# A transformer block on one core: token tiles combined in pairs, and the last sequence's weighted sums moved to TensorE

## The reference, cut to what matters

```
h = layernorm(x) * (1 + cb) + sb
top_logits, top_idx = top_k(h @ gate_w, 2)          # two experts per token
top_w = softmax(top_logits)
y_e   = silu(h @ w1[e]) @ w2[e]                     # for the two experts of a token
x = x + gb * (top_w[0] * y_first + top_w[1] * y_second)
```

## Time and profile before

| what | value |
|---|---|
| median of three executions | 990.87 us (990.5 to 992.32) |
| span of the profiled execution, first to last instruction | 985.5 us |
| mean granted TensorE clock | 0.975 |
| TensorE busy | 890.2 us (90%) |
| VectorE busy | 712.9 us (72%) |
| ScalarE busy | 580.1 us (59%) |
| GpSimd busy | 350.7 us (36%) |
| DMA, mean over the span | 112 GB/s |

### The profile page before, as it was taken

The page is one execution under the profiler, slowest core; times in us unless marked ns, Lnnn a source line. Parts: engine busy times, 40 slices in busy tenths (PEclk is TensorE's granted clock), DMA queues, the critical chain, the costliest instruction groups (busy, mean ns, idle before and its releaser), DMA issues.

```text
span 985.5 us, 19308 instructions
## 1 busy us (share of the span) xinstructions
PE 890.2 (90%) x6090; PEld 529.1 (54%) x6164; DVE 712.9 (72%) x2285; ACT 580.1 (59%) x1268; POOL 350.7 (36%) x311
## 2 busy tenths in 40 slices
PE   7899899998899999989999987888899999999990
PEld 4443335433535434544443453432798899999880
DVE  7898776879566889657689668899547575444588
ACT  3335676766676777586676757757535433333563
POOL 4200030530430324323023444024585465565530
PEclk8998999999999999999999999999999999999996
DMA  6484535525506336253464565105332323222699
GB/s 204 122 176 108 79 110 111 91 72 98 79 1 144 68 79 144 76 70 95 73 123 105 127 114 180 36 26 177 110 97 76 96 73 105 73 81 75 194 313 306
DMA packets 83235, 110.61 MB, mean 112 GB/s; under 512 B 15930, under 2 KB 56434, under 8 KB 83138
## 3 DMA queue, kind: packets, MB, share of 16 engines
q1 hardware_dynamic: 75234, 88.40, 38.2%
q0 software_dynamic: 6816, 18.62, 6.0%
q10 hardware_dynamic: 1088, 2.36, 0.6%
HBM read 69.42 MB, written 35.41 MB: 106 GB/s over the span
## 4 chain that ended last, share of the span: by engine, by line
PE 64%; DVE 17%; ACT 9%; issue 6%; POOL 3%; DMA 1%; another core or an unknown queue 1%; SPq 0%; ACTq 0%; DVEq 0%; POOLq 0%
PE PY L1608 10%; PE PO L1741 9%; PE PH L1608 9%; PE PM L1698 9%; PE PS L1721 8%; ACT PR L1073 3%; PE PHT L1826 3%; DVE MXF L1410 3%; DVE JK L1407 3%; PE PX L1753 2%; PE PX L1662 2%; PE PS L1725 2%; PE PX L1673 1%; PE PX L1770 1%; POOL SF L912 1%
## 5 line engine op out<-in xcount | busy, mean ns | idle before, releaser
L1073 ACT ACTIVATE PR<-PS 128x512 f32<-128x512 f32 (+3 forms) x768 | 335.3, 499 | 125.6 <-PE PS L1725 85.6
L1407 DVE CUSTOM_DVE_ANT_0 JK<-PM,MK 128x128 bf16<-128x128 f32 (+3 forms) x512 | 239.5, 485 | 54.9 <-PE PM L1698 52.5
L1698 PE MATMUL PM<-QK 128*128 128x512 bf16 (+3 forms) x725 | 234.3, 332 | 22.9 <-DVE MXF L1410 11.6
L1721 PE MATMUL PS<-QK 128*128 128x512 bf16 (+3 forms) x737 | 235.0, 330 | 11.7 <-ACT PR L1073 9.2
L1410 DVE TENSOR_REDUCE MXF<-PM 128x1 f32<-128x512 f32 x256 | 175.2, 684 | 76.8 <-PE PM L1698 61.0
L1721 PEld LDWEIGHTS PS<-QK 128*128 128x128 bf16 x768 | 75.5, 99 | 167.2 <-ACT PR L1073 105.3
L1741 PE MATMUL PO<-PR,V 128*17 128x512 f32 (+3 forms) x1536 | 162.3, 495 | 0.2 <-DVE MXA L1407 0.2
L1698 PEld LDWEIGHTS PM<-QK 128*128 128x128 bf16 x768 | 75.5, 98 | 94.7 <-DVE MXF L1410 33.6
L1608 PE MATMUL PY<-W2S,HT 128*128 x852 | 119.4, 289 | 2.6 <-issue 1.8
L1725 PE MATMUL PS<-MT,identb 128*128 128x128 bf16 x512 | 111.4, 220 | 1.6 <-issue 0.8
L1608 PE MATMUL PH<-W1S,XT 128*128 x426 | 111.7, 397 | 0.6 <-DVE W2S L1562 0.6
(11 more groups left out here) (282 smaller groups left out, 1159.2 us busy)
## 6 DMA issues: line engine op xcount, KB each, us to landing
QK<-SD SPq DMA_DIRECT2D x180, 128.0 KB
SD<-SP SPq DMA_DIRECT2D x42, 256.0 KB, 2.9
OP<-OS SPq DMA_DIRECT2D x64, 64.0 KB
LP<-LR SPq DMA_DIRECT2D x64, 64.0 KB
W1S<-in_w SPq DMA_DIRECT2D x8, 512.0 KB, 6.6
X<-XA SPq DMA_DIRECT2D x3, 1024.0 KB, 8.4
H2D<-XA SPq DMA_DIRECT2D x3, 1024.0 KB, 4.8
YG<-YT SPq DMA_DIRECT2D x12, 256.0 KB
```

The costliest lines, as they stand in the source:

```text
L1073: eng.activation(PR[:, slot, i, c0:512], PS[m % 3][:, c0:512], ACT.Exp, scale=0.25).then_inc(S["exp"].sem, 1)
L1407: eng.tensor_tensor_reduce(JK[:, jk % 2, 0:w], PM[m % 3][:, 0:w], MK[:, 512 - w:512], 1.0, -3.0e38, ALU.add, ALU.max, MXA[:, mb, h, qt:qt ...
L1698: eng.matmul(PM[m % 3][:, 0:128 * (k1 - k0)], QK[:, r, h, 0, qt * 128:(qt + 1) * 128], QK[:, r, h, 1, k0 * 128:k1 * 128], start=True, stop ...
L1721: last = eng.matmul(PS[m % 3][:, c0:512], QK[:, r, h, 1, j * 128:(j + 1) * 128], QK[:, r, h, 0, 512 * f + c0:512 * f + 512], start=True, s ...
```

## The change

Token tiles are taken in pairs for the combine: n now counts pairs, 0 to 11 for sequences 0 to 2 (`LAST` = 12) and 12 to 15 for the last one. One transfer reads the residual rows of both tiles (256 KB), one the four expert rows (512 KB), one writes both (256 KB). ScalarE and VectorE's weighted steps stay one instruction for each tile, the gate product and the residual sum cover both tiles at once (128x512). The ring has 5 buffers for pairs. The keys are new: `gat(n)` 58.5 + n, `comb(n)` 60 + n, `out_st(n)` 60.5 + n.

For the last sequence all residual rows come in one transfer (`xrl`, 1 MB, key 71), ScalarE builds 16 diagonal matrices with the weights (`diag`, key 73), and TensorE forms the weighted sums with them, four fp32 matmuls of 256 columns for each pair, into PSUM banks that the expert part has left; VectorE then does only the gate product and the residual sum. The four gathers of expert rows have key 74.

```diff
-    for n in range(3 * NT):
-        place(NL + 2.5 + 0.6 * n, one("gat", n))
-        place(NL + 4.5 + 0.6 * n, combine(n))
-    for n in range(3 * NT, B * NT):
-        place(NF + 2, one("gat", n))
-        place(NF + 8 + n - 3 * NT, combine(n))
+    for n in range(LAST):
+        place(NL + 2.5 + n, one("gat", n))
+        place(NL + 4 + n, combine(n))
+    place(NF, one("xrl"))
+    place(NF + 2, one("diag"))
+    for n in range(LAST, LAST + PAIR_N):
+        place(NF + 3, one("gat", n))
+        place(NF + 8 + n - LAST, combine(n))
...
-RING = 10
+RING = 5
+PAIR_N = NT // 2
+LAST = (B - 1) * PAIR_N
...
 SyncE, gat(n):
-                    sp.wait_ge(S[f"x2{b}"], 16)
-                    if RING <= n < 3 * NT:
+                    if RING <= n < LAST:
                         sp.wait_ge(*after(f"o{r}", "out_st", n - RING))
-                    if n == 3 * NT:
-                        sp.wait_ge(*after("fh", "up", NF - 1))
-                    eng.dma_start(XR[r][:, :], X2[b, 128 * (n % NT):128 * (n % NT) + 128, :]).then_inc(S[f"yg{r}"].sem, 16)
-                    store_wait(sp, NL if n < 3 * NT else NF)
-                    eng.dma_start(YG[r][:, :, :], YT[EMPTY + 256 * n:EMPTY + 256 + 256 * n, :].rearrange("(k p) d -> p k d", p=128)
+                    if n < LAST:
+                        sp.wait_ge(S[f"x2{b}"], 16)
+                        eng.dma_start(XR[r], pair_rows(X2, n)).then_inc(S[f"yg{r}"].sem, 16)
+                    store_wait(sp, NL if n < LAST else NF)
+                    eng.dma_start(YG[r], YT[EMPTY + 512 * n:EMPTY + 512 + 512 * n, :].rearrange("(k p) d -> p k d", p=128)
                                   ).then_inc(S[f"yg{r}"].sem, 16)
+                elif kind == "xrl":
+                    sp.wait_ge(S[f"x2{B - 1}"], 16)
+                    sp.wait_ge(*after("fh", "up", NF - 1))
+                    eng.dma_start(XRL[:, :, :], x2_tiles(B - 1)).then_inc(S["xrl"].sem, 16)
...
 ScalarE:
+                    for t in range(2):
+                        eng.activation(YG[r][:, 2 * t, :], YG[r][:, 2 * t, :], ACT.Copy,
+                                       scale=TW[:, 0, 2 * n + t:2 * n + t + 1]).then_inc(S["cmb_a"].sem, 1)
+                elif kind == "diag":
+                    ac.wait_ge(*after("wt", "weights", 1))
+                    ac.wait_ge(*after("fh", "up", NF - 1))
+                    for n in range(NT):
+                        for k in range(2):
+                            eng.activation(DG[:, n, k, :], ident[:, :], ACT.Copy,
+                                           scale=TW[:, k, 2 * LAST + n:2 * LAST + n + 1]).then_inc(S["dg"].sem, 1)
...
 VectorE, comb(n):
+                    if some:
+                        dv.wait_ge(*after("cmb_a", "comb", n))
+                        for t in range(2):
+                            eng.scalar_tensor_tensor(out=YG[r][:, 2 * t, :], in0=YG[r][:, 2 * t + 1, :], ...)
+                        dv.wait_ge(S["comb"], c + 2)
+                    else:
+                        dv.wait_ge(*after("wsum", "comb", n))
+                        dv.wait_ge(S["xrl"], 16)
+                    eng.tensor_tensor(first, first if some else WS[n - LAST].rearrange("p (t d) -> p t d", t=2), gate,
+                                      ALU.mult).then_inc(sem, 1)
+                    dv.wait_ge(*after("comb", "comb", n))
+                    eng.tensor_tensor(XR[r], first, XR[r], ALU.add).then_inc(S["cmb_d"].sem, 1)
...
 TensorE:
+                elif kind == "comb" and a[0] >= LAST:
+                    pe.wait_ge(*after("dg", "diag"))
+                    pe.wait_ge(*after(f"yg{r}", "gat", n))
+                    for t in range(2):
+                        for k in range(2):
+                            last = eng.matmul(WS[i][:, 256 * t:256 * t + 256], DG[:, 2 * i + t, k, :], YG[r][:, 2 * t + k, :],
+                                              start=(k == 0), stop=(k == 1))
+                    last.then_inc(S["wsum"].sem, 1)
```

More of the change, by code:

```diff
@@ L393 @@
     "ystore": {f"ys{i}": (lambda t, i=i: 16 * (t % 4 == i)) for i in range(4)},
-    "gat": {f"yg{i}": (lambda n, i=i: 32 * (gat_ring(n) == i)) for i in range(RING + NT)},
-    "comb": {"cmb_a": 1, "comb": 2, "cmb_d": lambda n: int(n not in LATE), "cmb_p": lambda n: int(n in LATE)},
-    "out_st": {f"o{i}": (lambda n, i=i: 16 * (gat_ring(n) == i)) for i in range(RING + NT)},
+    "gat": {f"yg{i}": (lambda n, i=i: (32 if n < LAST else 16) * (gat_ring(n) == i)) for i in range(RING + PAIR_N)},
+    "xrl": {"xrl": 16},
+    "diag": {"dg": 2 * NT},
+    "comb": {"cmb_a": lambda n: 2 * (n < LAST), "wsum": lambda n: int(n >= LAST), "comb": lambda n: 3 if n < LAST else 1, "cmb_d": 1},
+    "out_st": {f"o{i}": (lambda n, i=i: 16 * (gat_ring(n) == i)) for i in range(RING + PAIR_N)},
 }
@@ L539, in adaln_block @@
         end = ExitStack()
-        YG = [sb(f"YG{i}", [128, 2, D], F32, end) for i in range(4)]
-        XR = [sb(f"XR{i}", [128, D], F32, end) for i in range(4)]
+        YG = [sb(f"YG{i}", [128, 4, D], F32, end)[:, :, :] for i in range(2)]
+        XR = [sb(f"XR{i}", [128, 2, D], F32, end)[:, :, :] for i in range(2)]
         G3R = G3[:, :, :, :].rearrange("p b t n -> p (b t) n")
-        YG += [XB[:, 3 * i:3 * i + 2, :] for i in range(2)] + [G3R[:, 3 * i:3 * i + 2, :] for i in range(4)]
-        XR += [XB[:, 3 * i + 2, :] for i in range(2)] + [G3R[:, 3 * i + 2, :] for i in range(4)]
+        YG += [XB[:, 0:4, :], G3R[:, 0:4, :], G3R[:, 6:10, :]]
+        XR += [XB[:, 4:6, :], G3R[:, 4:6, :], G3R[:, 10:12, :]]
         end.close()
@@ L552, in adaln_block @@
         last = ExitStack()
-        YG += [sb(f"YGL{i}", [128, 2, D], F32, last) for i in range(NT)]
-        XR += [sb(f"XRL{i}", [128, D], F32, last) for i in range(NT)]
+        YG += [sb(f"YGL{i}", [128, 4, D], F32, last)[:, :, :] for i in range(PAIR_N)]
+        XRL = sb("XRL", [128, NT, D], F32, last)
+        XR += [XRL[:, 2 * i:2 * i + 2, :] for i in range(PAIR_N)]
+        DG = sb("DG", [128, NT, 2, 128], F32, last)
         last.close()
@@ L569, in adaln_block, with results @@
         pff.close()
+        WS = [PX[:, :], PXT[:, :, :].rearrange("p a n -> p (a n)"), PH[0][:, :], PH[1][:, :]]
+        def results(r, k):
+            return YG[r].rearrange("p (t k) d -> p t k d", k=2)[:, :, k, :]
         CD = nc.dram_tensor("CD", [NG, 96, 128], BF16).ap()
@@ L864, in gpsimd_program @@
             const = S["const"].sem
-            done = {n: 0 for n in ("const", "sub_p", "neg_p", "gbo", "div_p", "om", "bias", "h2", "both", "cmb_p")}
+            done = {n: 0 for n in ("const", "sub_p", "neg_p", "gbo", "div_p", "om", "bias", "h2", "both")}
             newest = []
@@ L1149, in scalar_program @@
                     eng.activation(YO[:, t % 4, :], PY[t % 2][:, 0:256], ACT.Copy).then_inc(S["yo_a"].sem, 1)
-                elif kind == "comb":
+                elif kind == "comb" and a[0] < LAST:
                     n = a[0]
```

46 lines of the change are left out of this document (19 added, 27 removed).

## The result

The changed kernel took 1003.74 us (median of four, 1000.16 to 1005.87), the kernel before 990.68 us (median of four beside it). The ratio is 1.013, 95% interval 1.0107 to 1.0152: slower by 13 us. The forecast was slower by 6.0 us, 996.9 us, with a range that ended at 1002.0. Direction and mechanism were right, the size was under half of what was measured.

What follows compares the result with a forecast made beforehand. TensorE's expert tiles, then some 24 us of combine, were taken to set the end. Adding 10.5 us for late expert tiles and taking off 4.5 for a shorter tail gave +6.0 us, 996.9 us; range 986.4 to 1002.0.

Steps and rivals of the forecast that it cites:

- What the pairs save: Combine: VectorE needs 2.4 us for a pair instead of 2.6; counted at nothing while TensorE is the bound.
- What the new order costs: Combine loop: a round trip of 8.6 us against two beats, 6.96 us, makes a beat 4.3 us instead of 3.48.
- issue to landing: Combine loop: time from the issue of a pair's 512 KB gather until it lands, taken as 4.3 us.
- The signs that the prediction named: Changed timeline: `up(t)` every 4.2 to 4.4 us, ScalarE waiting for `YG<-YT`, TensorE idle some 8 us.
- the bound from above: Combine loop: upper estimate for a 512 KB gather's landing, from loaded 256 KB gathers, 5.3 to 6.2 us.
- The DMA rate as a reason of its own: Combine loop: a beat moves 1.05 + 0.26 MB, 3.8 us at 345 GB/s, already over 3.48.
- Where that puts the expert tiles: End of the expert tiles: last `down` ends at 971.8 us against 961.25 before, 10.5 us late.
- The tail: Behind the last `down`: scatter, gathers, TensorE's four pairs and store take 19.7 us instead of 24.2.
- From span to time: Whole run: 5.4 us added to the trace's end at 991.5 us gives a run's time, 996.9 us.
- number 4: Loop landings near the upper rows, 5.3 us, giving 1001.9 us, or tail clock staying low, 1001.4; chance 0.23 together.

Runs made afterwards that it cites:

- experiment 10: Changed kernel with a lead of four pairs and 34 dummy matmuls between the last `down` and the first diagonal matmul: 988.21 us, ratio 1.0005.
- experiment 7: Changed kernel with the twelve pairs' residual reads and result stores shrunk to 16 bytes a row, output of three sequences left out: 997.9 us, ratio 1.0089.
- experiment 11: experiment 10 with the last sequence's 1 MB of residual rows issued one place earlier in SyncE's list: 985.36 us, ratio 0.9975 to the kernel before.
- experiment 8: experiment 6 with 32 dummy matmuls between the last `down` and the first diagonal matmul: 993.37 us, ratio 1.0053 to the kernel before.
- experiment 6: Changed kernel with a pair combined every 1.2 beats and 3.6 beats of lead: 994.93 us, ratio 1.0061 to the kernel before.

## Why the prediction was right or wrong

**What the pairs save:** right in size. VectorE's group for a pair measures 0.88 us for the two weighted sums and 0.69 for each of the 128x512 instructions, 2.3 us with gaps. It brought nothing that shows: against 2.6 us for two single tiles it saves 0.3 us in a round trip of 10.

**What the new order costs:** the mechanism was right, and two experiments show it from both sides: one pair more of lead takes 8 us off the changed kernel, and a shorter lead alone puts 12 us on the old one. The step that failed is one term of the sum for the round trip, "issue to landing", put at 4.3 us. It measured 5.8 us in the mean. With it the round trip is 0.9 + 5.8 + 3.4 = 10.1 us, and the trace has it so: `comb(0)` ends at 925.57 and `comb(10)` at 976.40, five round trips of 10.2; `comb(1)` at 930.09 and `comb(11)` at 979.57, five of 9.9. Forecast were 926.3 and 969.3, 929.8 and 972.8. The starts were right within 0.8 us, and the 1.5 us of the term, five times over, are the 7 us at the end.

```profile
924.88 0.69 DVE L1623 TENSOR_TENSOR XR<-YG,XR 128x512 f32<-128x512 f32 x1
...
975.71 0.69 DVE L1623 TENSOR_TENSOR XR<-YG,XR 128x512 f32<-128x512 f32 x1
```

These are the last instructions of `comb(0)` and `comb(10)`. The signs that the prediction named came out accordingly: `up(t)` comes every 4.65 us in the mean from `up(60)` to `up(70)`, in steps of 3.2 to 8.7 us, instead of every 4.2 to 4.4; TensorE's waits for VectorE are 14.2 us instead of some 8; ScalarE does wait for DMA `YG<-YT`.

Why the term was short: I took the fixed part of a transfer, 1.4 us, from a 128 KB write into DRAM, and it does not hold for a gather from `YT`. In the tail the first 512 KB, with three more of its kind behind it, lands 987.76 - 983.74 = 4.0 us after its issue; if the bytes take 1.5 us, 2.5 are fixed, by this estimate. No run separates the two parts. The experiment without stores and residual rows has 4.5 in the loop. The row that I had put down as the bound from above (5.3 to 6.2 us, from the loaded gathers of the earlier trace rows) was the one that held. I had chosen near the lower end since an empty queue was the nearest state; but with expert gathers and scatters under way it never is. The page "DMA: Bandwidth & Descriptors" of the Trainium skill (Anatomy of one DMA) gives 2.0 us for the fixed part, in a fit for transfers issued by GpSimd. These gathers are issued by SyncE, which the prediction did not say where it used the fit. With the tail's 4.0 us the trace is over the estimated 3.2 us of that fit too.

**The DMA rate as a reason of its own** ("the beat cannot be kept either way"): wrong. With a lead of four pairs two profiles keep 3.48 us from pair to pair with the DMA share at 0.98 to 1.04, at 321 to 351 GB/s. So the 345 GB/s was no bad figure. The sum of 3.8 us a beat left out that with more lead the reads of four pairs are issued before the first combine, at 917.3 to 921.0 us in experiment 10 against a first scaling at 924.2, so that the twelve pairs spread over more than twelve beats.

**Where that puts the expert tiles:** 10.5 us late forecast, 18.8 measured, 8.3 more. The five rounds of 10.2 us instead of 8.6 are 7.8 of them; 0.7 go off again, as `comb(0)` ended that much earlier than forecast; and 1.2 come on top, since the last `down` ran at the lower clock after 4.66 us of waiting (2.90 us instead of 1.68). That stalls in the loop bring the clock down in the loop itself (0.87 and 0.89 in the stretches above) was not in the working.

**The tail:** forecast 19.7 us, measured 21.1. The scatter's 2.5 us, `diag`'s 4.8 us (5.3 forecast, covered as forecast), the four pairs' 9.2 us (9.5 forecast, 3.5 for the first), VectorE's last two and the store (2.65 us) came as worked out; the clock was at 0.50 when the first diagonal matmul started and at 1.00 for the last pairs. Too short were the first gather again (4.0 instead of 2.9 us) and the scatter's issue, 0.8 us after the eviction instead of 0.1. The comparison with the old tail was wrong in kind: I set the new tail against the 24.2 us of the kernel before, whose gathers stood behind the unfinished combines of sequence 2. With pairs that are through by then, the old tail takes 21.15 us as well (21.5 with a lead of four). The 3 us belong to the order, not to TensorE.

**From span to time:** I added 5.4 us and took them for what lies outside the span, but they are the difference between a median and the span of another execution. Where both are known for one execution it is 2.4 us (1003.5 and 1001.1), and 1.8 to 1.9 us in the runs of the kernel before beside the experiments. So the profiled execution of before was a short one, some 987.4 us by this estimate. Part of my error in the span, 9.6 us, was hidden by this; against the median it is 6.8. The 2.8 us between the two are luck.

**The rivals:** the one that came out is number 4, landings near the upper rows, and the run went beyond it. Its price, 1001.9 us, used 5.3 us; the range ended there, although 6.2 was written as the bound.

## What to carry to other kernels

A ring of buffers is worth only the lead with which its transfers are let go: count how many beats lie between the step that a load stands behind in its queue and the step that needs it, and set that against the whole round trip, store, issue, landing and the engines' own instructions. Where that trip closes on itself, an error in one landing time is multiplied by the number of rounds, so take the landing from rows under the same load, and let the range reach to the highest of them. When work moves to TensorE behind an idle stretch, count it at the lower clock, and compare it with the old way in the new order, not in the old one.

## What the runs showed of the hardware

- A 512 KB read of 1 KB rows from DRAM was used by an engine 4.0 us after its issue in the tail of the changed kernel, with only three more such reads behind it; 4.5 us in the mean beside the expert gathers and scatters (experiment 7); 5.8 us in the mean, 4.55 to 7.7, with 512 KB more ahead of it (changed kernel).
- A busy DMA share is not bytes: in the changed kernel it was 0.81 from 928 to 929 us while 68 GB/s were moved, and 1.10 at 392 GB/s three microseconds later.
- In experiment 10 TensorE's granted clock was 1.00 when the first diagonal matmul came, after 1.93 us of waiting, then 0.50 from 974 to 977 us, and 1.00 again from 978. In experiment 11, with 1.45 us of waiting, it stayed at 1.00. One profile of each was taken, so what decides is open.
- 34 dummy matmuls in the wait of the tail gave 2.1 us of faster matmuls in the changed kernel (7.2 instead of 9.2 us for the four pairs); the 32 that ended 6.95 us before the work (experiment 8) gave nothing, 9.3 us for the four pairs against 9.2 in experiment 6.
